# A Mamba-2 mixer inside a fused decoder layer: who adds the residual, where the squares run, and in what order the gated output is split

## What is computed

```python
residual = hidden_states
h = rmsnorm(hidden_states, norm_w)
h = mamba2_mixer(h, in_proj_w, conv_w, conv_b, dt_bias, A_log, D, ssm_norm_w, out_proj_w)
h = residual + h
...
# inside the mixer: z, xBC, dt = split(u @ in_proj_w.T); conv + silu on xBC
# state scan over the sequence (16 heads of 64, state 128)
y = rmsnorm(y * jax.nn.silu(z), ssm_norm_w)
return jnp.einsum('ble,de->bld', y, out_proj_w)
```

## Time and profile before

| | us |
|---|---|
| median of 3 runs | 2724.34 |
| lowest to highest run | 2722.08 to 2725.27 |
| the profiled execution's own time | 2722.0 |
| its span (first to last instruction) | 2720.2 |
| one looped mixer round | about 101.1 |

### The profile page before, as it was taken

How to read it: one execution, slowest core, us unless ns; L and a number is a source line. 1 busy time by engine, 2 the same in 40 slices (tenths; PEclk the granted TensorE clock), 3 DMA queues, 4 the chain that set the end, 5 groups by cost and what they waited for, 6 DMA issues and landing times.

```text
span 2720.2 us, 42348 instructions
## 1 busy us (share of the span) xinstructions
PE 2659.7 (98%) x15264; PEld 2070.4 (76%) x15264; DVE 1523.4 (56%) x2561; ACT 1019.5 (37%) x2375; POOL 693.8 (26%) x594
## 2 busy tenths in 40 slices
PE   7999999999999999999999989999999999999999
PEld 5777777777778888888888867777777777777776
DVE  8787797797795322332233277777777774111122
ACT  6334334334434222122212255555555553222221
POOL 6553553553561101000100101322233322000000
PEclk9999999999999999999999999999999999999999
DMA  4001001101114101110111211110111124211111
GB/s 154 27 21 47 31 15 46 44 3 46 46 48 140 62 1 62 62 62 0 62 62 48 73 70 48 63 40 29 62 54 62 58 64 150 82 47 46 46 46 47
DMA packets 85482, 147.83 MB, mean 54 GB/s; under 512 B 4032, under 2 KB 17984, under 8 KB 85408
## 3 DMA queue, kind: packets, MB, share of 16 engines
q1 hardware_dynamic: 85408, 146.84, 15.7%
HBM read 113.27 MB, written 33.55 MB: 54 GB/s over the span
## 4 chain that ended last, share of the span: by engine, by line
PE 88%; DVE 8%; issue 2%; ACT 1%; DMA 1%; DVEq 0%; SPq 0%; POOL 0%; ACTq 0%; POOLq 0%
PE ps L75 22%; PE ps L77 22%; PE ps L76 22%; PE ps L1770 4%; PE ps L2133 4%; PE ps L816 2%; PE ps L1782 2%; PE ps L1761 2%; DVE mx_m L608 1%; DVE mx_cv L600 1%; PE ps L792 1%; PE ps L804 1%; PE ps L747 1%; PE ps L1714 1%; PE ps L844 1%
## 5 line engine op out<-in xcount | busy, mean ns | idle before, releaser
L1471 ACT ACTIVATE at_pr<-ps,at_nm 128x256 f32<-128x256 f32 x512 | 235.6, 473 | 201.7 <-DVE at_nm L1621 201.7
L1162 DVE TENSOR_TENSOR gm_m_lo<-gm_m,gm_m_hi 128x512 fp32r<-128x512 f32 (+1 forms) x88 | 61.1, 694 | 416.9 <-ACT gm_m_hi L1079 416.9
L75 PE MATMUL ps<-sh_u_hi,gm_gu_hi 128*128 128x512 f32 (+1 forms) x704 | 274.9, 390 | 0.0
L76 PE MATMUL ps<-sh_u_lo,gm_gu_hi 128*128 128x512 f32 (+1 forms) x704 | 274.8, 390 | 0.0
L77 PE MATMUL ps<-sh_u_hi,gm_gu_lo 128*128 128x512 f32 (+1 forms) x704 | 274.7, 390 | 0.0
L1627 DVE COPY at_pT<-ps 128x512 f32<-128x512 f32 x256 | 176.3, 689 | 138.5 <-PE ps L1770 136.4
L1073 ACT ACTIVATE gm_sg<-ps 128x512 f32<-128x512 f32 (+1 forms) x88 | 52.7, 599 | 517.6 <-PE ps L77 517.4
L543 POOL TENSOR_TENSOR mx_m<-mx_m,mx_g 128x512 f32<-128x512 f32 x128 | 185.4, 1448 | 86.3 <-DVE mx_m L610 86.1
L75 PE MATMUL ps<-sh_u_hi,qm_w_hi 128*128 128x512 f32 x512 | 201.6, 394 | 2.1 <-issue 1.1
L77 PE MATMUL ps<-sh_u_hi,qm_w_lo 128*128 128x512 f32 x512 | 199.6, 390 | 0.0
L76 PE MATMUL ps<-sh_u_lo,qm_w_hi 128*128 128x512 f32 x512 | 199.4, 389 | 0.0
(11 more groups left out here) (252 smaller groups left out, 6352.6 us busy)
## 6 DMA issues: line engine op xcount, KB each, us to landing
sh_xf<-x_scratch SPq DMA_DIRECT2D x16, 1024.0 KB, 7.5
mx_xr<-in_x SPq DMA_DIRECT2D x8, 1024.0 KB, 5.6
h_scratch<-mx_xr SPq DMA_DIRECT2D x8, 1024.0 KB, 5.1
sh_xf<-h_scratch SPq DMA_DIRECT2D x8, 1024.0 KB, 8.4
gm_xr<-in_x SPq DMA_DIRECT2D x8, 1024.0 KB, 7.3
gm_r<-h_scratch SPq DMA_DIRECT2D x8, 1024.0 KB, 6.1
x_scratch<-gm_r SPq DMA_DIRECT2D x8, 1024.0 KB, 5.2
at_cf<-in_ctxT SPq DMA_DIRECT2D x16, 512.0 KB, 3.9
```

Of the source, the lines that this page charges most:

```text
L75: nc.tensor.matmul(out, l_hi, r_hi, start=first, stop=False)
L76: nc.tensor.matmul(out, l_hi, r_lo, start=False, stop=False)
L1471: A(pr[h][:, t, :], SC[h][:, SEQ * t:SEQ * t + SEQ], ACT.Exp, bias=nm[:, 4 * n + h, t:t + 1], accum_out=sums[:, 2 * b + t, 4 * g + h:4 * g ...
```

## The change

It has four parts.

1. **Residual.** In all rounds but the last, DVE's four scaled adds are gone. ACT copies each output bank from PSUM with the factor `rg` into the buffers `m0` (`scale_out`, semaphore `ho`), two at the round's end and two behind the first `tap` of the next round, and GpSimd adds them to `xr` (`h1`). `conv_in(i, 2..5)` each wait for one `ho`; the round's first scan waits for `h1`, since it writes `m0`.
2. **Squares in the loop.** The four `square(i+1, t)` move from the convolution part to ACT's passes `j` = 0 to 3; GpSimd's `first(i+1)` moves behind head 9; the four `norm(i+1, t)` move from passes 1 to 4 to passes 5 (two) and 6 (two).
3. **Low half first.** `g_low(i, j-1)` moves ahead of both scans of its pass.
4. **Spreading later.** `spread(i, 2j+4)` moves behind `chunk_out(i, j-1)`.

```diff
--- before.py
+++ after.py
@@ -343,9 +343,12 @@
     wt = Weights(nc, su, places, pieces, lambda n: n if n < IN_PIECES else IN_PIECES + n % TT, IN_PIECES)
 
     names = ("x0 xr st dtp dtc dtt in G dat bc zp xt y out ss a nab ee u ln c rec c2 sp dt dta da dah dal "
-             "dac tap cv sl Ge z xd sc M t g gs glo acc sse rg h1").split()
+             "dac tap cv sl Ge z xd sc M t g gs glo acc sse rg ho h1").split()
     s = {**sh.s, **{k: sem(f"mx_{k}") for k in names}}
     me.s = s
+
+
+    OUT = (2, 3, 0, 1)
 
     def ahead(i):
 
@@ -462,6 +465,14 @@
             act.wait_ge(s["u"], i + 1)
             A(d["ln"], d["u"], ACT.Ln).then_inc(s["ln"], 1)
 
+        def scale_out(i, n):
+
+            t = OUT[n]
+            act.wait_ge(s["out"], KI * i + KI)
+            act.wait_ge(s["y"], KI * i + KI)
+            act.wait_ge(s["rg"], i + 1)
+            A(m0[t][:, :], ps[t][:, :], ACT.Copy, scale=rg[:, t:t + 1]).then_inc(s["ho"], 1)
+
         def main(i):
             if step_0(i):
                 take_dt(i)
@@ -469,6 +480,9 @@
             tap(i, 0)
             if step_0(i):
                 exp_ln(i)
+            else:
+                scale_out(i - 1, 2)
+                scale_out(i - 1, 3)
             tap(i, 1)
             act.wait_ge(s["dta"], i + 1)
             A(d["da"], d["dta"], ACT.Exp).then_inc(s["da"], 1)
@@ -484,8 +498,6 @@
                 silu(i, n - 1)
                 if step_0(i):
                     wt.high(act, min(3 * KD + 2 * (n - 1), IN_PIECES))
-                if n >= 5:
-                    square(i + 1, n - 5)
             silu(i, NCONV - 2)
             zsilu(i, 0)
             tap(i, NCONV - 1)
@@ -504,14 +516,19 @@
                 else:
                     at(act, s["acc"], 7 * i + j - 1)
                 A(acc[:, :] if j == 0 else sq[:, :], zs[j % 2][:, :], ACT.Square).then_inc(s["gs"], 1)
-                if 1 <= j <= TT:
-                    norm(i + 1, j - 1)
+                if j < TT:
+                    square(i + 1, j)
+                elif j in (5, 6):
+                    norm(i + 1, 2 * j - 10)
+                    norm(i + 1, 2 * j - 9)
                 if final(i) and j >= 1:
 
                     me.nxt.wt.high(act, j if j <= 4 else 4 + 2 * max(j - 5, 0))
             if not final(i):
                 take_dt(i + 1)
                 exp_ln(i + 1)
+                scale_out(i, 0)
+                scale_out(i, 1)
 
         first(0)
         steps(act, main)
@@ -536,7 +553,6 @@
 
                 pool.wait_ge(su.small, smalls)
                 wt.by_pool(pool, len(pieces))
-            first(i + 1)
             pool.wait_ge(s["Ge"], 2 * i + 2)
             for h in range(NH):
                 pool.wait_ge(s["sc"], NH * i + h + 1)
@@ -544,10 +560,17 @@
                 G(m1[h % 4][:, :], m1[h % 4][:, :], g1[:, :], ALU.mult).then_inc(s["M"], 1)
                 if h % 2 == 1 and h >= 5:
                     add_squares(i, (h - 3) // 2)
+                if h == 9:
+                    first(i + 1)
             add_squares(i, 7)
-            at(pool, s["h1"], TT * i)
+            at(pool, s["ho"], TT * i)
             pool.wait_ge(s["sse"], i + 1)
             G(rg[:, :], v0[:, :], mhalf[:, :], ALU.pow).then_inc(s["rg"], 1)
+            if not final(i):
+                pool.wait_ge(s["xr"], 16 * i + 16)
+            for n, t in () if final(i) else enumerate(OUT):
+                pool.wait_ge(s["ho"], TT * i + n + 1)
+                G(xr[:, t, :], xr[:, t, :], m0[t][:, :], ALU.add).then_inc(s["h1"], 1)
 
         pool.wait_ge(su.dve, dve_0 + 4)
         first(0)
@@ -603,6 +626,9 @@
         def scan(i, h):
 
             dve.wait_ge(s["bc"], NH * i + h + 1)
+            if h == 0:
+
+                at(dve, s["h1"], TT * i)
             at(dve, s["y"], KI * i + h // 2 - 1)
             bank = BC[h % 2]
             V.tensor_tensor_scan(m0[h % 4][:, :], bank[:, :], eye0[:, :], 0.0, ALU.mult, ALU.add)
@@ -691,10 +717,10 @@
             if step_0(i):
                 wt.low(dve, IN_PIECES)
             for j in range(KI):
+                if j >= 1:
+                    g_low(i, j - 1)
                 if j + 1 < KI:
                     scan(i, 2 * j + 2)
-                if j >= 1:
-                    g_low(i, j - 1)
                 if j == KI - 1:
                     split(i + 1, 0)
                     split(i + 1, 1)
@@ -721,10 +747,12 @@
             V.tensor_scalar(v0[:, :], Y[:, 0:TT], 1.0 / DI, RMS_EPS, ALU.mult, ALU.add).then_inc(s["sse"], 1)
             if not final(i):
                 dt_second(i + 1)
-            dve.wait_ge(s["out"], KI * i + KI)
-            dve.wait_ge(s["xr"], 16 * i + 16)
-            dve.wait_ge(s["rg"], i + 1)
-            for t in range(TT):
+            if final(i):
+
+                dve.wait_ge(s["out"], KI * i + KI)
+                dve.wait_ge(s["xr"], 16 * i + 16)
+                dve.wait_ge(s["rg"], i + 1)
+            for t in range(TT) if final(i) else ():
                 V.scalar_tensor_tensor(xr[:, t, :], ps[t][:, :], rg[:, t:t + 1], xr[:, t, :], ALU.mult,
                                        ALU.add).then_inc(s["h1"], 1)
 
@@ -764,10 +792,10 @@
         def conv_in(i, n, also=None):
             if step_0(i) and n % 4 == 2:
                 pe.wait_ge(*wt.lows(n // 4 * KD + 2 * KD - 1))
+            if 2 <= n <= 5:
+                at(pe, s["ho"], TT * (i - 1) + n - 1)
             if n >= 4:
                 pe.wait_ge(s["cv"], 3 * NCONV * i + 3 * (n - 3))
-            elif n == 2:
-                at(pe, s["h1"], TT * i)
             project(CB[n], E_X + P * CH[n], also).then_inc(s["in"], 1)
 
         def z_in(i, c):
@@ -896,10 +924,10 @@
                 else:
                     turn(i + 1, 2)
                     turn(i + 1, 3)
+                if j >= 1:
+                    chunk_out(i, j - 1)
                 if j + 2 < KI:
                     spread(i, 2 * j + 4)
-                if j >= 1:
-                    chunk_out(i, j - 1)
             if final(i):
                 chunk_out(i, KI - 1)
             else:
```

## The result

The changed kernel takes 2736.23 us (median of 6 runs, 2735.84 to 2737.23) against 2724.35 for the kernel before (6 runs, 2721.6 to 2725.27): 11.9 us more, ratio 1.0046, 95% interval 1.0033 to 1.0059. The forecast was 2733, range 2727 to 2740, so it came out 3 us short of the measured time.

A forecast was written before the change was run, and what follows sets the result against it. PE, busy 98% of the span, was taken to bound the kernel. Seven rounds of 1.68 - 0.45 (8.6) plus 0.9 in the last gave +9.4 us; on 2722.0, with 2.3 for the median, the forecast was 2733, range 2727 to 2740.

The forecast's parts named there:

- Part 1, 0: Residual by ACT's copies and GpSimd's adds: all in time for `conv_in` and the first scan, so 0 us.
- The waits of pass 1: `turn_x(2)` 0.74 us earlier, `z_in(3)` then held by `scale_x(2)`: gain 0.45 a round; 0.88 ahead of `chunk_y(1)` stays.
- Later passes, 0: After pass 1, DVE waits some 0.7 us for `g`'s high half, a shorter `g_low` can repay it; PE loses 0.
- The norms, 1.68 a round: Two norms behind pass 6's high half on ACT make PE wait 1.68 us a round at `turn(i+1, 0)`.
- The sum, +9.4: Seven rounds of 1.68 - 0.45 give 8.6 us, the last round 0.9: together 9.4 us slower.
- Rival 1: Pass 1: the wait of `chunk_y(1)` for GpSimd's products goes too, 7.0 us less, 2726.5; chance 0.12.
- Rival 2: DVE's whole chain comes earlier, pass 1's waits and the one at `turn` go: gain 15 us, 2709; chance 0.07.
- Rival 3: Pass 1: GpSimd blocks `g_low(0)` (1.5 us instead of 0.66), delaying `z_in(3)`: 6.7 more, 2740; chance 0.10.

The follow-up runs named there:

- part1_alone: The kernel before with only the residual by ACT's scaled copies and GpSimd's adds: 2723.07 us, ratio 0.9998.
- parts34: The kernel before with the low half ahead of the scans and the spreading behind the output product, squares and norms as before: 2722.38 us, ratio 0.9996.
- norms5_scalex: norms_pass5 with `scale_x(j+1)` put ahead of D*x + y on DVE in every pass: 2722.23 us, ratio 0.9992.
- norms_pass5: The changed kernel with all four norms in pass 5 instead of two in pass 5 and two in pass 6: 2722.73 us, ratio 0.9997 to the kernel before.
- part2_alone: The kernel before with only the squares moved to passes 0 to 3 and the norms to passes 5 and 6: 2737.65 us, ratio 1.0046.
- norms_3_1: The changed kernel with three norms in pass 5 and one in pass 6: 2731.17 us, ratio 1.0029 to the kernel before.
- parts34_scalex: parts34 with `scale_x(j+1)` put ahead of D*x + y on DVE: 2717.94 us, ratio 0.9975 to the kernel before.
- part4_alone: The kernel before with only the spreading moved behind the output product: 2723.41 us, ratio 0.9999.
- open_pass1: parts34 with `conv(9)` behind pass 0's low half, `scale_x(2)` between pass 1's scans, `silu(9)` behind `zsilu(2)`: 2721.99 us, ratio 0.9993 to the kernel before.
- pass1_reordered: The kernel before with open_pass1's moves in pass 1 only, low half between the scans from pass 2 on: 2722.55 us, ratio 0.9993.

## Why the prediction was right, step by step

- **Part 1, 0.** Right in the time, 0.07 short in the timeline: part1_alone.
- **The waits of pass 1.** Right: `turn_x(2)` was expected at 0.2 to 0.3 and waits 0.25; `z_in(3)` kept 0.44 of the expected 0.45; `chunk_y(1)` stayed, within 0.07. `z_in(3)` starts 0.54 behind the spreading where 0.23 is usual, so it waits the expected 0.3, and it starts 0.06 after the end of `scale_x(2)`. That `scale_x(2)` holds it is shown by parts34 (a wait of 0.34 for it) and norms5_scalex, where it is gone.
- **Later passes, 0.** Right within 0.1 a round. DVE now idles for ACT's high half, but the low half takes 0.69 where its median was 1.42, and no pass of the looped rounds after pass 1 waits for DVE:

```profile
L651 DVE TENSOR_TENSOR mx_g_lo<-mx_zs,mx_g_hi x64: 678/692/694, 67.9 to 839.5; 128x512 fp32r<-128x512 f32 x64
its engine sat idle before it (us, times) until:
  ACT mx_g_hi L513: 36.4, 52
```

- **The norms, 1.68 a round.** Right: 1.71 in the round shown, confirmed by taking both norms out (norms_pass5), by adding them to the kernel before (part2_alone) and by taking out one (norms_3_1). In the last round the transposes wait 1.48, and the wait of 0.35 behind them is gone, as the prediction had it.
- **The sum, +9.4.** The net per round was put at 1.23 and is 1.61. The two large terms are right; what was missing is small terms that I had set to 0. Each is read from the starts of PE's instructions in one looped round:

| term | expected | in the changed kernel | the experiment |
|---|---|---|---|
| norms: transposes later | 1.68 | 1.71 | part2_alone 1.70 |
| the same: one more loss between the transposes and `chunk_y(7)` | 0 | 0.06 | part2_alone 0.06 |
| pass 1: `chunk_y(1)` to `z_in(3)` | -0.45 | -0.44 | parts34 -0.46 |
| pass 1: `z_in(3)` to `chunk_y(2)`, the restart behind the new wait | 0 | 0.13 | parts34 0.15; 0.03 in parts34_scalex, where `z_in(3)` does not wait |
| part 1, at `chunk_y(1)` | 0 | 0.07 | part1_alone 0.07 |
| part 4, passes 2 to 6 | 0 | 0.08 | part4_alone 0.09 |
| sum | 1.23 | 1.61 | |

Six looped rounds give 9.7 of the measured 11.9 and the last one about 1.1 by the profile (0.9 expected). Round 0 is 2.2 longer there, but part of that is the lower clock, so its own share is not known. Why a restart costs this, and why part 4 costs 0.02 a pass, stays open.
- **Rivals.** Rival 1 did not occur: the wait for GpSimd stayed. Rival 2, DVE's freed time pulling everything forward, did not either: the high half of pass 6 starts 0.16 earlier in the round than before (88.42 against 88.58 us behind the last product), which is just what PE had gained by then. The scan of the odd head still waits for PE's spreading in that pass (1.07). Rival 3, a blocked `g_low`, is the opposite of what happened; all 64 took 0.69 at most.

By the Trainium skill (SBUF — State Buffer, Who interferes with whom) the second of two such instructions waits for the first; the trace agrees, 1.42 in the median when `g_low` ran among GpSimd's products and 0.69 when it ran in the gap behind them.

## What to carry to other kernels

When the bound engine has almost no idle time, a move is worth little more than the wait that it removes, and it costs whatever it takes beyond the slack that its result had. So for each moved instruction find its reader on the bound engine and what now stands directly ahead of it: here the norms had two passes of slack, and two of them, 0.61 each, ended behind a result that arrives only 0.80 us before PE reads them. A wait that is removed also uncovers the next one in the chain, often in the same pass (`scale_x` behind `zsilu`) or one pass later (open_pass1, pass1_reordered). The follow-up that was read off the new chain paid most: swapping two instructions of DVE turned a change worth 2 us into one worth 6. And a wait costs more than the profile lists for it: 1.56 listed were 1.76 in the round.

## What was not expected of the hardware

- Waiting for the producer cost DVE no more than running beside GpSimd did. Moving the low half right behind its producer made DVE idle 0.70 us ahead of it, and each run became 0.73 shorter (1.42 to 0.69); GpSimd's 128x512 product fell as well, from a mean of 1448 ns to 1286:

```profile
L559 POOL TENSOR_TENSOR mx_m<-mx_m,mx_g 128x512 f32<-128x512 f32 x128 | 164.5, 1286 | 256.7 <-DVE mx_m L636 256.7
```

- The lower clock in round 0 of the changed kernel's profiled execution. PE stood for 2.82 us; in the stand its granted clock fell (0.91 from 55 to 56 us), and behind it the clock was 0.50, the lower of its two levels (1.2 of 2.4 GHz), for some 6 us of unbroken work. Matmuls of 512 columns started 0.43 us apart instead of 0.23. The spreading that ended the stand:

```profile
56.46 0.80 PE L832 MATMUL ps<-mx_daT,mx_sel 128*128 128x512 f32 x1 [2.82 <-DVE mx_m L636]
```

and the stretch behind it (length, busy us and count of each engine, granted clock, DMA share, GB/s):

```profile
56.50:62.50 6.00, 6.00 (x14) 4.47 (x14) 5.93 (x9) 0.72 (x2) 3.88 (x4) 0.50 0.00 0
```

The kernel before waited 2.6 us at a spreading of round 0 and kept 1.00. The dip does not go with the loss: the granted clock from 30 to 70 us is 0.91 in the changed kernel, in norms_3_1 and in parts34 (and parts34 is not slower than before), 0.96 in seven of the other profiles and 1.00 in four.
